# First attention of a fused network: diagonal blocks gathered in two units without their zero quarters

## The reference, cut to what matters

```python
sim = einsum('bhid,bhjd->bhij', q, k) * SCALE
sim = SOFTCLAMP * tanh(sim / SOFTCLAMP)
sim = where(causal, sim, finfo.min)      # query i sees keys j <= i
attn = softmax(sim, axis=-1)
out = einsum('bhij,bhjd->bhid', attn, v)
out = out.transpose(0, 2, 1, 3).reshape(b, n, H * DH) @ Wo.T
```

## Time and profile before

| | |
|---|---|
| median of 3 runs | 1223.57 us |
| the profiled execution | 1226.15 us, span 1224.4 us |
| TensorE busy in the span | 1129.5 us (92%) |
| VectorE, ScalarE, GpSimd busy | 856.5, 704.5, 522.8 us |
| mean granted TensorE clock | 0.969 |
| first attention, 66 to 428 us: TensorE busy | 348.64 of 362 us, clock 1.00 |
| the same stretch: VectorE, ScalarE, GpSimd | 262.01, 270.62, 230.96 us |

### The profile page before, as it was taken

One profiled execution on the slowest core, in us unless ns is written; L12 is line 12 of the kernel. 1 busy time (PEld: TensorE's weight loads), 2 busy tenths in 40 slices (PEclk: granted clock), 3 DMA queues, 4 the chain that ended last, 5 costly groups with the idle time before them and its releaser, 6 DMA issues. The chain is left out here.

```text
span 1224.4 us, 29054 instructions
## 1 busy us (share of the span) xinstructions
PE 1129.5 (92%) x10981; PEld 631.5 (52%) x10981; DVE 856.5 (70%) x1805; ACT 704.5 (58%) x915; POOL 522.8 (43%) x529
## 2 busy tenths in 40 slices
PE   3899999999999898879997999999999999788998
PEld 1456556566566585359983222222222222546996
DVE  6457767777777655874425899999999993585442
ACT  3587777777777525512225177777777778451220
POOL 0056666665666600337862114223322321035883
PEclk9799999999999998879999999999999999797999
DMA  4000110010010110516752211222222110223665
GB/s 128 1 9 20 27 42 18 24 42 18 24 42 19 27 30 1 176 59 173 197 94 89 75 43 54 62 58 57 61 57 54 54 51 18 92 88 116 182 171 122
DMA packets 60345, 81.83 MB, mean 67 GB/s; under 512 B 23488, under 2 KB 41284, under 8 KB 59612
## 3 DMA queue, kind: packets, MB, share of 16 engines
q1 hardware_dynamic: 48180, 70.54, 19.0%
q0 software_dynamic: 10880, 8.86, 4.9%
q10 hardware_dynamic: 1192, 1.19, 0.3%
HBM read 55.12 MB, written 15.72 MB: 58 GB/s over the span
## 5 line engine op out<-in xcount | busy, mean ns | idle before, releaser
L2020 ACT ACTIVATE at_PR<-psum 128x1024 f32<-128x1024 f32 x256 | 248.0, 1021 | 106.8 <-PE psum L2267 104.8
L2089 DVE TENSOR_REDUCE at_MX<-psum 128x1 f32<-128x512 f32 x468 | 298.2, 684 | 11.5 <-PE psum L2239 8.9
L511 ACT ACTIVATE PR<-psum 128x1024 f32<-128x1024 f32 x144 | 145.7, 1022 | 83.1 <-PE psum L841 74.7
L860 PE MATMUL psum<-PR,V 64*64 64x256 f32 (+1 forms) x2560 | 171.7, 357 | 5.1 <-issue 1.5
L841 PE MATMUL psum<-Q,K 64*64 64x512 f32 (+2 forms) x1792 | 151.5, 437 | 2.1 <-ACT PR L511 2.1
L860 PEld LDWEIGHTS psum<-PR,V 64*64 64x64 f32 x2560 | 96.9, 133 | 102.3 <-issue 90.4
L516 ACT ACTIVATE PR<-PR 128x1024 f32<-128x1024 f32 x144 | 143.8, 1051 | 0.0
L2284 PE MATMUL psum<-at_PR,at_VG 128*32 128x512 f32 x1024 | 136.2, 604 | 0.8 <-POOL at_PR L1957 0.8
L488 POOL TENSOR_SCALAR_AFFINE_SELECT PR<-PR 128x256 f32<-128x256 f32 (+1 forms) x80 | 57.1, 719 | 168.4 <-ACT PR L516 167.6
L1549 PE MATMUL psum<-moe_XGT,moe_WE 128*128 128x256 f32 x512 | 124.6, 388 | 0.2
L1957 POOL TENSOR_TENSOR at_PR<-at_PR,at_FAC 128x512 f32<-128x512 f32 x64 | 81.1, 1268 | 101.5 <-ACT at_PR L2020 101.5
(11 more groups left out here) (267 smaller groups left out, 1853.4 us busy)
## 6 DMA issues: line engine op xcount, KB each, us to landing
moe_WE<-in_c_We SPq DMA_DIRECT2D x32, 768.0 KB, 4.6
XB<-at_r_dram SPq DMA_DIRECT2D x32, 256.0 KB, 3.8
at_outs_dram<-at_OTS SPq DMA_DIRECT2D x15, 256.0 KB, 3.0
moe_rows_dram<-XNS SPq DMA_DIRECT2D x2, 1152.0 KB, 11.4
moe_spare_dram<-moe_zeros SPq DMA_DIRECT2D x2, 1024.0 KB, 13.9
moe_sum_dram<-XB SPq DMA_DIRECT2D x2, 1024.0 KB, 3.8
moe_SG<-moe_spare_dram SPq DMA_DIRECT2D x8, 256.0 KB
at_KU<-in_c_max_krows SPq DMA_DIRECT2D x16, 128.0 KB
```

The costliest lines, as they stand in the source:

```text
L511: act.activation(PR[u][:, :, :], S[(b + u) % 2][:, :, :], ACT.Tanh, scale=SCALE0 / CLAMP).then_inc(z.clamped, 1)
L860: mm = pe.matmul(O[row[h], q:q + w], V[rows, b, j, row[h]], PR[u][rows, h, at:at + w], start=(first and u == 0), stop=(not first and u == ...
L2020: act.activation(PR[:, gu % PRS, 2 * r:2 * r + 2, :].rearrange("p h n -> p (h n)"), g.psum[:, 2 * r * BANK:(2 * r + 2) * BANK], ACT.Exp).t ...
L2089: dve.tensor_reduce(MX[:, c // 32 % 2, 8 * (c % 2) + 4 * pair + I % 4, khalf:khalf + 1], bank(("max", c))[:, :], AX, ALU.max).then_inc(z.r ...
```

## The change

`BLOCKS` is dealt anew: the eight diagonal blocks fill units 4 and 8, and the other seven units hold none. For a diagonal block, the second half of the keys sees only the second half of the queries, so a quarter of the block is zero. In units 4 and 8, `scores` and `multiply` leave that quarter out: the matmuls of the second key half run over 64 columns and the others over 128. For the key blocks 0, 1, 6 and 7 the two key halves are stored swapped (`SWAPPED`, in K, V and the projection of V), so that in a diagonal unit the wide and the narrow matmuls fall to different tiles. Tanh, exp and the adds still go over the whole unit; the quarter that has no scores holds old values of S until the mask sets it to zero.

A diagonal unit is masked in two instructions: a select over its four unswapped blocks (both heads) and a multiplication of its four swapped blocks by a matrix TRI of zeros and ones, which three further GpSimd instructions make at the start. The masks of units 0, 3, 5 and 6 go. `ADDS` has 11 entries in place of 10, over the same 3840 columns: unit 0 has none, unit 1 has one of 512, unit 4 a copy and an add, unit 8 two adds of 256. `clamp` waits for adds by the table `READ_LAST`. The unit with four different key blocks, 16 score matmuls of 128 columns, is unit 7 in place of 5; units 5 and 6 have 8 of 256.

```diff
-BLOCKS = [[(0, 2), (0, 3), (0, 0), (0, 1)], [(0, 4), (0, 5), (0, 6), (0, 7)], [(1, 2), (1, 3), (1, 6), (1, 7)],
-          [(2, 2), (2, 3), (2, 6), (2, 7)], [(3, 4), (3, 5), (3, 6), (3, 7)], [(3, 3), (5, 5), (1, 1), (7, 7)],
-          [(4, 4), (4, 5), (4, 6), (4, 7)], [(1, 4), (1, 5), (5, 6), (5, 7)], [(2, 4), (2, 5), (6, 6), (6, 7)]]
+BLOCKS = [[(0, 2), (0, 3), (0, 6), (0, 7)], [(1, 2), (1, 3), (1, 6), (1, 7)], [(2, 4), (2, 5), (2, 6), (2, 7)],
+          [(3, 4), (3, 5), (3, 6), (3, 7)], [(2, 2), (3, 3), (0, 0), (1, 1)], [(0, 4), (0, 5), (4, 6), (4, 7)],
+          [(1, 4), (1, 5), (5, 6), (5, 7)], [(2, 3), (4, 5), (0, 1), (6, 7)], [(4, 4), (5, 5), (6, 6), (7, 7)]]
+SWAPPED = (0, 1, 6, 7)
...
-DIAGS = [[n * P for n, (j, i) in enumerate(u) if j == i] for u in BLOCKS]
-ADDS = [[(256, slice(2, 3), (0, slice(1, 2)), None)],
-        [],
-        [(256, slice(0, 1), (0, slice(0, 1)), (2, slice(0, 1))), (256, slice(3, 4), (1, slice(1, 2)), (2, slice(1, 2)))],
-        [(256, slice(0, 4, 3), None, (3, slice(0, 2)))],
-        [(256, slice(1, 2), (1, slice(0, 1)), (4, slice(0, 1))), (256, slice(3, 4), None, (4, slice(1, 2)))],
-        [(128, slice(1, 8, 2), None, (5, slice(0, 4)))],
+DIAGS = [all(j == i for j, i in u) for u in BLOCKS]
+MASKS = 2
+ADDS = [[],
+        [(256, slice(0, 4, 3), (0, slice(0, 2)), (1, slice(0, 2)))],
+        [(256, slice(3, 4), None, (2, slice(1, 2)))],
+        [(256, slice(1, 2), (2, slice(0, 1)), (3, slice(0, 1))), (256, slice(3, 4), None, (3, slice(1, 2)))],
+        [(128, slice(4, 6), (4, slice(1, 4, 2)), None), (128, slice(0, 2), None, (4, slice(0, 4, 2)))],
+        [(256, slice(1, 4, 2), None, (5, slice(0, 2)))],
         [(256, slice(1, 4, 2), None, (6, slice(0, 2)))],
-        [(256, slice(1, 4, 2), None, (7, slice(0, 2)))],
-        [(256, slice(1, 4, 2), None, (8, slice(0, 2)))]]
+        [(128, slice(1, 8, 2), None, (7, slice(0, 4)))],
+        [(128, slice(2, 4), None, (8, slice(0, 4, 2))), (128, slice(6, 8), None, (8, slice(1, 4, 2)))]]
+READ_LAST = [1, 1, 3, 3, 4, 5, 6, 7, 8]
...
+        def half(j, c):
+            return 1 - c if j in SWAPPED else c
+        def keys(j, c):
+            return j * P + DH0 * half(j, c)
...
-            if u == 0:
+            if u == 1:
                 wait(eng, z.totalled, s - 1)
...
-                    whole = len(DIAGS[u]) == 4
-                    blocks = v if whole else v[:, DIAGS[u][0] // P::4, :]
-                    last = pool.affine_select(out=blocks, in_=blocks, compare_op=ALU.is_ge, fill=0.0, base=0,
-                                              pattern=[[0, 8 if whole else 2], [1, P]], channel_multiplier=-1)
-                    last.then_inc(z.masked, 1)
+                    pool.affine_select(out=v[:, 0::2, :], in_=v[:, 0::2, :], compare_op=ALU.is_ge, fill=0.0, base=0,
+                                       pattern=[[0, 4], [1, P]], channel_multiplier=-1).then_inc(z.masked, 1)
+                    pool.tensor_tensor(v[:, 1::2, :], v[:, 1::2, :], bcast(TRI[:, :].unsqueeze(1), [P, 4, P]), ALU.mult
+                                       ).then_inc(z.masked, 1)
...
-                    through = ADDED[max(u, 4) + 1] - ADDED[NU]
+                    through = ADDED[READ_LAST[u] + 1] - ADDED[NU]
...
+                    if DIAGS[u]:
+                        for n in range(2):
+                            for (j, at, q, w), tiles in ((near[n], (0, 1)), (far[n], (1, 0))):
+                                for c in tiles:
+                                    from_ = DH0 * half(j, c)
+                                    for h in range(2):
+                                        mm = pe.matmul(S[(b + u) % 2][row[c], h, at + from_:at + w],
+                                                       K[row[h], b, keys(j, c):keys(j, c) + DH0], Q[row[h], b, q + from_:q + w],
+                                                       start=True, stop=True, skip_group_check=True)
+                        mm.then_inc(z.scored, 1)
+                        return
...
-                            rows = row[side if first != swap else 1 - side]
+                            part = side if first != swap else 1 - side
+                            rows = row[part]
                             for j, at, q, w in PIECES[u][side][n:n + 1]:
+                                from_ = DH0 * half(j, part) if DIAGS[u] else 0
                                 for h in range(2):
-                                    mm = pe.matmul(O[row[h], q:q + w], V[rows, b, j, row[h]], PR[u][rows, h, at:at + w],
+                                    mm = pe.matmul(O[row[h], q + from_:q + w], V[rows, b, j, row[h]], PR[u][rows, h, at + from_:at + w],
```

More of the change, by code:

```diff
@@ L295, in runs @@
     return found
-PIECES = [(runs(u[0:2], 0), runs(u[2:4], 2 * P)) for u in BLOCKS]
+PIECES = [([[u[0][0], 0, ORDER.index(u[0][1]) * P, P], [u[1][0], 2 * P, ORDER.index(u[1][1]) * P, P]],
+           [[u[2][0], P, ORDER.index(u[2][1]) * P, P], [u[3][0], 3 * P, ORDER.index(u[3][1]) * P, P]])
+          if all(j == i for j, i in u) else (runs(u[0:2], 0), runs(u[2:4], 2 * P)) for u in BLOCKS]
 NU = len(PIECES)
-DIAGS = [[n * P for n, (j, i) in enumerate(u) if j == i] for u in BLOCKS]
-ADDS = [[(256, slice(2, 3), (0, slice(1, 2)), None)],
-        [],
-        [(256, slice(0, 1), (0, slice(0, 1)), (2, slice(0, 1))), (256, slice(3, 4), (1, slice(1, 2)), (2, slice(1, 2)))],
-        [(256, slice(0, 4, 3), None, (3, slice(0, 2)))],
-        [(256, slice(1, 2), (1, slice(0, 1)), (4, slice(0, 1))), (256, slice(3, 4), None, (4, slice(1, 2)))],
-        [(128, slice(1, 8, 2), None, (5, slice(0, 4)))],
+DIAGS = [all(j == i for j, i in u) for u in BLOCKS]
[6 more added lines that the diff above has]
+        [(256, slice(1, 4, 2), None, (5, slice(0, 2)))],
         [(256, slice(1, 4, 2), None, (6, slice(0, 2)))],
-        [(256, slice(1, 4, 2), None, (7, slice(0, 2)))],
-        [(256, slice(1, 4, 2), None, (8, slice(0, 2)))]]
+        [(128, slice(1, 8, 2), None, (7, slice(0, 4)))],
+        [(128, slice(2, 4), None, (8, slice(0, 4, 2))), (128, slice(6, 8), None, (8, slice(1, 4, 2)))]]
+READ_LAST = [1, 1, 3, 3, 4, 5, 6, 7, 8]
 ADDED = [sum(len(a) for a in ADDS[:u]) for u in range(NU + 1)]
-MASKED = [sum(1 for d in DIAGS[:u] if d) for u in range(NU + 1)]
+MASKED = [MASKS * sum(DIAGS[:u]) for u in range(NU + 1)]
 ROWS = 32
@@ L336, in stage_front @@
      z.multiplied, z.taken, z.summedA, z.summedB, z.totalled, z.copied, z.spread, z.inverted, z.kept, z.broad, z.scaled, z.wo, z.summed, z.added, z.passed,
-     z.halved, z.part_projected) = (
+     z.halved, z.part_projected, z.triangle) = (
         sem("at0_" + x) for x in (
@@ L340, in stage_front @@
         "totalled copied spread inverted kept broad scaled wo summed added passed "
-        "halved part_projected").split())
+        "halved part_projected triangle").split())
     with ExitStack() as tmp:
@@ L355, in stage_front @@
         RC = sb("RC", [P, 2, BT])
+        TRI = sb("TRI", [P, P])
         r_dram = nc.dram_tensor("at0_r_dram", [2, SEQ], F32).ap()
@@ L395, in unit_done @@
             if DIAGS[u]:
-                eng.wait_ge(z.masked, MASKED[NU] * s + MASKED[u] + 1)
+                eng.wait_ge(z.masked, MASKED[NU] * s + MASKED[u] + MASKS)
             else:
@@ L500, in _ @@
                 pool.memset(g.ones[:, :], 1.0).then_inc(z.ones, 1)
+                pool.memset(TRI[:, :], 1.0).then_inc(z.triangle, 1)
+                pool.wait_ge(z.triangle, 1)
+                pool.affine_select(out=TRI[row[0], :], in_=TRI[row[0], :], compare_op=ALU.is_ge, fill=0.0, base=-DH0,
+                                   pattern=[[1, P]], channel_multiplier=-1).then_inc(z.triangle, 1)
+                pool.wait_ge(z.triangle, 2)
+                pool.affine_select(out=TRI[row[1], 0:DH0], in_=TRI[row[1], 0:DH0], compare_op=ALU.is_ge, fill=0.0, base=0,
+                                   pattern=[[1, DH0]], channel_multiplier=-1).then_inc(z.triangle, 1)
+                pool.wait_ge(z.triangle, 3)
                 span(pair)(pool)
@@ L788, in project_first @@
                             for c in range(2):
-                                first = k % 2 * BANK + t * P + DH0 * c
+                                first = keys(4 * (k % 2) + t, c)
                                 mm = pe.matmul(J[k % 2][row[c], t * P:(t + 1) * P], g.XT[:, first:first + DH0],
@@ L816, in project @@
                                 else:
-                                    at = b * SEQ + x * BANK + t * P + DH0 * c
+                                    at = b * SEQ + keys(4 * x + t, c)
                                     mm = pe.matmul(J[x][row[c], t * P:(t + 1) * P], g.XT[rows, at:at + DH0], W[rows, 2, :],
@@ L840, in scores @@
                                     of = split(Q[row[h], b, :], 2 * P)[:, q // (2 * P)::(far[0][2] - q) // (2 * P), :]
-                                mm = pe.matmul(into, K[row[h], b, j * P + DH0 * c:j * P + DH0 * (c + 1)], of,
```

(1 more changed line is left out.)

## The result

The changed kernel takes 1271.22 us (median of four, 1269.49 to 1273.85) against 1222.82 for the kernel before (1221.6 to 1228.06): ratio 1.0377, 95% interval 1.035 to 1.0405, that is 48 us more. The direction was forecast, the size was not: +12.9 forecast, range up to 1248.

The account below looks back on a forecast made before the run. TensorE was taken as the bound, with VectorE 0 to 1.2 us behind it at four meetings a turn. The terms 12.6 + 5.6 - 5.6 + 1.4 - 1.1 gave +12.9 us, so 1236.5 us, range 1214 to 1248.

Parts of the forecast that it names:

- it is columns that cost: TensorE's matmuls: time goes by columns; a quarter less in units 4 and 8 saves 13.8 us at the streaming price.
- Unit 7 gets 16-way pieces in place of unit 5: no change: TensorE's work: moving the 16-way pieces to another unit was priced at nothing.
- A, totals at step 5: First batch's totals wait for VectorE's V copies behind turns with GpSimd: +1.8 us a turn, 7 turns, 12.6 us.
- B: VectorE's take at step 10, behind unit 1's new add: +0.7 us a turn, 8 turns, 5.6 us; TensorE idle about 1.
- D: VectorE's take at step 1, behind the same new add: +0.2 us a turn, 7 turns, 1.4 us.
- C, totals at step 14: Second totals, masks of units 5 and 6 gone from GpSimd: -0.8 us a turn, 7 turns, -5.6 us; wait under 0.6.
- The forecast's own sign: TensorE's idle time in the 362 us stage grows by some 27 us, 13 for delay, 14 for work gone.
- The last turn: The last turn's 1.08 us wait for unit 5's big mask goes: -1.1 us.
- Prices: Scores of units 4 and 8 about 0.65 us, narrow half 0.22; select about 0.6, multiply 1.27.
- The rivals: Saving comes through, 1210 (0.10); GpSimd leaves gaps, 1215 (0.18); both totals meetings cancel, 1226 (0.15); worse, 1249 (0.12).

Follow-up runs that it names:

- after_unrolled: The changed kernel with TensorE's loop over the head pairs written out eight times: 1243.77 us, ratio 1.0129.
- after_both_in_loop: The changed kernel, loop kept, with scale two steps later and the take ahead of the adds on VectorE: 1237.7 us, ratio 1.0128.
- before_unrolled: The kernel before with TensorE's loop written out eight times: 1227.6 us, ratio 1.0.
- before_204: The kernel before with two units' value matmuls cut into 128-column pieces, same columns, 1754 instructions in TensorE's loop body: 49 us more than before.
- before_228: The kernel before with five units' value matmuls cut into 128-column pieces, same columns, about 1946 instructions a turn: 1247.09 us, ratio 1.0148.
- experiment 5: 128 semaphore increments put ahead of TensorE's loop, in before_204 (1259.04 us, ratio 1.0269) and in the changed kernel (1286.37 us, ratio 1.0511).

## Why the prediction was right or wrong

**The step that failed** is the first line of the change part by part: "it is columns that cost", and with it "Unit 7 gets 16-way pieces in place of unit 5: no change". I priced matmuls by columns, and nowhere counted them. The change puts 160 more matmuls and 160 more weight loads into TensorE's loop body, and that carries it over the size up to which the chip keeps it. The page of the kernel before gave the warning, had I asked: q8 with 59 packets in all, and none in the loop. Its price is 33 of the 48 us (after against after_unrolled, each against its own runs of before).

The Trainium skill, "Runtime: NRT & Kernel Launch", section "Instruction fetch mechanics", would have led there: it says that TensorE's store holds 2048 instructions, is filled in blocks of 256, and that a taken branch to a page outside the window of two pages stops the engine until it is fetched. The stops of 2.5 to 3.5 us at the loop's head agree with such a stop. The figure of 2048 doesn't carry over as a limit for a loop: 1690 were already fetched anew every second turn, 1625 were not. The same section speaks of two cache lines; a body of 1625 instructions, more than six times 256, stayed without one packet in 230 us, so the measurement speaks against that for TensorE.

**A, totals at step 5: right.** Scale ends at 213.3, copy 1.38 us, two adds of 1.5 to 1.6, V at 217.73, wait 2.13 us (said: 1.5 to 2.5), in after_unrolled, and 2.04 in the changed kernel itself. Less the 0.4 us of work saved in front of it, that is +1.7 a turn, +1.8 in the sum.

**B and D, takes: right in sum, the split not.** TensorE of after_unrolled idles 0.70 us at B in every turn of the loop against 0.3 us before, where I said about 1. D was put at nearly nothing; it stands 1.0 to 1.2 us in four of the seven turns (the row at 299.01 follows a take that ends at 298.90) and not at all in the others. Taking the add out of the way of all 15 takes gives back 6 us, where the sum has 7.0.

**C, totals at step 14: nearly right.** The wait is 0.68 us in after_unrolled (1.20 before; "under 0.6" was said). In the changed kernel itself it is 0.6 or less, and gone in most turns.

**The clock: left out of the sum.** The turn of after_unrolled that has full clock and no wait at D is 46.4 us long (219.15 to 265.56), against 45.7 before and 45.4 in the undisturbed turns of before_unrolled: 0.7 to 1.0 us for A, B and C together, where the forecast has 1.7. Another 6.5 us come from the lowered clock behind A's wait; the forecast has no term for it. So it is in part luck that the sum of 12.9 lies so near the 16 measured. The forecast's own sign, 27 us more of idle time on TensorE, says the same: from the first batch-0 totals to the last the idle time grows by 18 us in after_unrolled (13.3 to 31.5), and TensorE is busy 302.6 us for 304.5 before, although a clean half turn has 0.7 us less of work.

**The last turn: wrong by 2.6 us.** The wait for the mask went, as forecast, but the last value matmuls now wait 1.45 us for an exponent, and the turn is 1.5 us longer, not 1.1 shorter; 0.7 of that is the last take (2.17 us of idle time against 1.47).

**Prices.** A diagonal unit's scores take 0.67 us (213.31 to 213.98; said 0.65), and 16 matmuls of 64 columns 0.23 us (213.98 to 214.21; said 0.22), 14 ns each. The floor of about 25 ns that the Trainium skill gives ("TensorE: Matmul & The Clock Gate", section "Wait — 56ns, not 53.3ns?") therefore doesn't hold from start to start where four 64x64 tiles run at once. The select over four blocks takes 0.64 us and the multiply 1.28 (said 0.6 and 1.27).

**The account.** Of 48 us, 16 remain without the loop: the queues, and the clock behind their waits (forecast 13). The other 33 are the fetched loop; after_both_in_loop puts it at 26, and whether the 7 between them are real is open. If they are, the clock may have a part: between 111 and 426 us it was granted at 0.94 in the changed kernel, 0.98 in after_both_in_loop, 0.97 in after_unrolled and 1.00 before. Open as well is why one body has stops in mid-body and another hardly any (up to 10 us a turn in before_204, from 3 in before_228); experiment 5 shows only that the body's place has a part in it. The rivals all moved times about in the queues. None was about instructions, so the range of 1214 to 1248 could not reach the result, though it holds the time of the same change without its loop.

## What to carry to other kernels

Count the instructions that a change adds to each engine's loop body, as well as its columns and bytes, and look whether the instruction queue is silent inside the loop; if it is, the body's size is a resource with an edge, and its place may count too. A tight loop near that edge should be written out (free here) before anything else is tried. When work is regrouped, follow each copy that TensorE waits for through its queue: here moving one scale two slots and a take ahead of an add was worth 27 us, and the columns saved 13.8 at most. And price a wait by more than its length: the clock can be lower for some us after it.

## What the runs showed of the hardware that was not expected

- A loop of about 1625 TensorE instructions stays in the store, one of 1690 is fetched anew every second turn, one of 1754 every turn, or every second turn if 128 instructions are put ahead of it. The count of pages touched, 7 or 8, would fit as well.
- A fetched turn moves 9 packets of 16384 bytes and costs 3 to 10 us: 2.5 to 3.5 us at the loop's head, in some kernels shorter stops in mid-body, and often half clock soon after the stop (8 matmuls of 512 columns in 1.99 us in place of 1.07).
- After a wait of 2.13 us for VectorE, TensorE's clock was 0.93 over the next half turn in four turns of six, at 1.6 us each.
- Straight-line code of the same size isn't held up: 1.0 [0.9982, 1.0019] for the kernel before written out.
- 128 semaphore increments in a row on TensorE's queue held it for 18.6 us.
- Matmuls of 64 columns on four tiles started every 14 ns.
